# First attention: two of the six additions that sum the weighted shifts are made by GpSimd beside VectorE's next products

## The chip, the cores and the metric

The kernel runs on one core of one Trainium2 chip. The metric is the device time in microseconds, as the median of several runs. The profile is of one execution; its span goes from the first to the last instruction.

## The reference

Two decoder layers with post-norm work on x of 32 sequences by 128 positions by 256 channels: `x = layernorm(x + sublayer(x))`, six times. The sublayers are a windowed attention, a cross attention and routed experts in the first layer, and a decayed attention, a memory attention and a quantized feed-forward network in the second. The change touches the first one:

```
Q, K, V = heads(wq), heads(wk), heads(wv)          # 16 heads of 16 channels
Kw, Vw = Kp[:, :, idx], Vp[:, :, idx]              # 7 shifts, -3 to 3, zero padded
attn = softmax(einsum('bhld,bhlwd->bhlw', Q, Kw) / sqrt(16))
fw = attn * conn                                   # conn: a softmax over the 7 shifts, from weights alone
fw = fw / (fw.sum(-1) + 1e-9)
out = einsum('bhlw,bhlwd->bhld', fw, Vw)
return out @ wo.T + bo
```

So `out` is, for each position, the sum of seven shifted copies of V, each weighted by head.

## The kernel before

The 32 sequences are cut into 16 groups of two. A group's x is 128 positions by 2 x 256 numbers. Each sublayer is a "station", a Python generator that runs once per group on each engine: A (windowed attention, `windowed`), B (`cross`), X (`experts`), C (`decayed`, with the choice of the memory), E (`memory`), F (`feed_forward`); S is the setup. Each `yield` ends a step. The order in which an engine takes the steps of the stations is written out by hand as a string of letters in `ORDER`, one per engine; `walk` goes through it. All instructions of an engine run in this order, so a wait in one step holds up everything behind it. In the middle of the kernel a group is in each station at once: while group 10 is in A, group 7 is in C.

Engines wait for each other by counters (semaphores). `own` is an engine's counter of its own instructions; an instruction that reads what an earlier one on the same engine wrote waits for it.

The first attention on VectorE (`windowed` in the vector block) has these parts. L990 multiplies Q with the seven shifts of K. L1005 to L1023 make the seven weights per head, in `e0`. Then `SUM_STEPS` names 13 steps. A step with one number, as `(3,)`, is L1034: it multiplies the shifted copy `vw[:, wi, :]`, 128 x 512 numbers, with its weights, in place. I call this product wi. A step with two numbers, as `(3, 0)`, is L1038: it adds copy 0 to copy 3. The sum ends up in copy 3 (`PAD`), and the last step raises `a_summed`, for which TensorE's transposes of it (L550) wait. `vw` and all other areas named area_... lie in SBUF; names with bank are in PSUM.

Around these steps in VectorE's queue stand steps of the other stations: of F L1263 and L1257 (two inputs from SBUF), L1284 and L1295 (an input from PSUM); of C the two instructions of L874, which add a bank to x and form the sums for the norm (`n_c.added`); of E L1198 and L1202, for whose result TensorE's next transposes wait.

GpSimd has, besides memsets in the setup, one step per station and group: `scales`, four instructions of 128 x 2 numbers (L1587, L1589, L1591, L1593) that turn the sums (`n.added`, from VectorE) and the squares (`n.squared`, from ScalarE) into the scale and shift of the norm, which ScalarE waits for.

Of the kernel before, what the change touches and what calls it, by code (L numbers as in the profile page):

```python
# [11 lines left out]
ALU = mybir.AluOpType  # L12
# [11 lines left out]
DH = D // H  # L24
# [31 lines left out]
SUM_STEPS = ((3,), (0,), (2,), (3, 0), (4,), (3, 2), (6,), (3, 4), (1,), (3, 6), (5,), (3, 1), (3, 5))  # L56
# [26 lines left out]
        "SAAAAAAASASSSAAAAAAAAAAAAAASSAAAAAABAASSABBAAAAAAAAAAAAAAXSAXSXAAAAASAAXBAXAAAAAAAAAXAAAAABBXSAXXXAAAAAX"  # L83
        "BBAAXBXAAAAAAAACAAAAAXCACAAXCXCAAAAAXEEEEEABABXBAAXEAAAAACAAXAAAACCAAXEECAFCXEEAAAAEFXEFFEBAXFFABAFFXBFF"
        "AFFFXAECFFAAFACCAFXAAAAAAEFAFFAAFEXCAFCFEEXAEAEFAXFAXEBFAFFAABFFXBFAFFFFXAECFFAAFACCAXAFAAAAEAAAAFFFFECX"
        "AFCFEEXAEAFEAXFAXEFBAFFAAFFBXBFAFFFFXAECFFAAFACCAAXFAAAAEAAFAFAFEFCXAFCFEEXAEAFXEAFABFEXAFFAAFFXBBFFAFFF"
        "XAECFFAAAFCCAXFAAAAAEAAAFAFFFEXCAFCFEEXAEAFXEFAAEFAFBFXAAFFXBBFFAFFFXAECFFAAAFCCAXAFAAAAEAAFAFAFFXECAFCF"
        "EEXAEAFXEEFAABXFAFFAAFFXBBFFFAFFXAECFFAAACFCXAAFAAAAEAAAFAFFFXECAFCFEEXAEAFXEFAEAXFFBAFAAFFXBBFFFFAFXAEC"
        "FFAAAFCCAXFAAAAAEAAAFAFFXFECAFCFEEXAEAFEXFAEAXFABAFFAFFXBBFAFFFFXAECFFAAACFCAXFAAAAAEAAAFAFFXFECAFCFEEXA"
        "EAXFEFAAEXFABAFFAFFXBBFAFFFFXAECFFAAACFAXCAFAAAAAEAAAFFXFFECAFCFEEXEAAFEXFAABEFFAAXAFFXFBBFAFFFFXAECFFAA"  # L90
        "AFCCXAFAAAAAEAAAFAFFXFECAFCFEEXEAAFEAXFXAEFABFFAAFFXBBFFAFFFXAEFCAFAAFXCCAFAAAAAEAFAAAFFFXECAFCFEEXEEFXE"
        "FBXFFBFFXFBFFFFFXEFXFFCFCCXEFFFFEFCFCXEEFEEEFFXXFFFCFFFFFXFEXFFCCFXFFFFFEXECFCFEEEEEFFCFFFFCEFCFFFFFFFEF"
        "CFEFCFFFEEFFEEEFFFFFFFFEFFFFFFFEFFFFFEFFFFFFFFFFFFFFFFFFFFFFF"
# [16 lines left out]
        "ABABXABXCABCXEABCEXAFBCEXAFBCEXAFBCEXAFBCXEAFBCXEAFBCXEAFBCEXAFBCXEAFBCEXAFBCXEAFBCXEFCXEFCEFEFF"  # L110
# [43 lines left out]
def build(nc, io, out):  # L154
    ctx = ExitStack()
    with ctx:
# [145 lines left out]
        a_summed, a_values, a_oT, a_wo = sems("a_summed a_values a_oT a_wo")  # L302
# [565 lines left out]
        def _(dve):  # L868
            own = Steps(dve_own)
# [116 lines left out]
            def windowed(g):  # L986
# [43 lines left out]
                for step in SUM_STEPS:  # L1030
                    if len(step) == 1:
                        (wi,) = step
                        v4 = vw[:, wi, :].rearrange("p (b h d) -> p b h d", b=GB, h=H)
                        made[wi] = own.mark(dve.tensor_tensor(v4, v4, bc(e4[:, :, wi, :], 3, DH), ALU.mult))  # L1034
# [546 lines left out]
        def _(pool):  # L1581
# [13 lines left out]
            def windowed(g):  # L1595
                scales(n_a, g).then_inc(n_a.scaled, 1)
                yield
# [120 lines left out]
```

## Time and profile before

| | us |
|---|---|
| median of 3 runs | 1125.49 |
| lowest and highest | 1124.31, 1127.63 |
| span of the profiled execution | 1122.6 |
| busy: TensorE, VectorE, ScalarE, GpSimd | 969.1, 943.0, 750.2, 140.0 |

In the rows PE is TensorE, PEld its weight loads, DVE VectorE, ACT ScalarE, POOL GpSimd. The table by stretches has: the stretch, its length, then for PE, PEld, DVE, ACT and POOL the busy time with the number of instructions, then the granted clock of TensorE as a share of full speed, the share of the DMA engines and GB/s. A row of the view in order of time has: start, duration, engine, line, operation, output and inputs, sizes, how many in a row are merged in it, and in brackets how long the engine was idle before it and what ended that. An instruction may start before the one ahead of it has ended. The chain of work that ended last is followed back from the last instruction, at each step to what released it or to the instruction before it on its engine.

### The profile page before, as it was taken

How to read it: one execution, taken by the hardware profiler on the slowest of the kernel's cores; microseconds unless marked ns; L12 is line 12 of the kernel's file. 1: busy time of each engine (PE TensorE's matmuls, PEld its weight loads, DVE VectorE, ACT ScalarE, POOL GpSimd, SP SyncE). 2: the span in 40 equal slices, each digit the busy share in tenths (PEclk: the TensorE clock that was granted, in tenths of full speed). 3: DMA queues.
4: the chain of work that ended last, by engine and by line, in shares of the span. 5: the costliest groups of instructions: out<-in, count | busy, mean ns of one | idle time of the engine just before them, and what ended most of it. 6: DMA issues, size and time to landing. Idle time of an engine off the chain costs nothing.

```text
span 1122.6 us, 19705 instructions
## 1 busy us (share of the span) xinstructions
PE 969.1 (86%) x7038; PEld 695.0 (62%) x7038; DVE 943.0 (84%) x2503; ACT 750.2 (67%) x1854; POOL 140.0 (12%) x401
## 2 busy tenths in 40 slices
PE   5768879999999999999999999989999888786552
PEld 3545657666767676767676676757576666564331
DVE  4799766689898989899999989898989886868854
ACT  2223454758696878778687868786868786767643
POOL 2000110101111020202020111111020201011000
PEclk8879899999999999999999999999999998999865
DMA  7832023011111212020303020211202000000000
GB/s 205 319 105 75 22 63 94 1 56 30 56 49 38 66 29 75 20 85 10 94 10 94 9 85 11 66 38 39 66 30 66 17 3 20 1 20 1 10 10 10
DMA packets 36626, 58.90 MB, mean 52 GB/s; under 512 B 6784, under 2 KB 15872, under 8 KB 36016
## 3 DMA queue, kind: packets, MB, share of 16 engines
q1 hardware_dynamic: 36528, 57.64, 16.7%
q8 instruction: 56, 0.92, 0.3%
q14 instruction: 42, 0.34, 0.1%
HBM read 28.65 MB, written 4.19 MB: 29 GB/s over the span
## 4 chain that ended last, share of the span: by engine, by line
DVE 52%; PE 31%; ACT 12%; issue 4%; POOL 1%; DMA 0%; SPq 0%; ACTq 0%; DVEq 0%; POOLq 0%
PE bank_c L444 9%; DVE area_f L1248 8%; PE bank_a L444 6%; PE banks_e L444 5%; DVE area_a L990 4%; DVE area_a L1034 4%; DVE neg_top L1181 4%; DVE area_f L1239 3%; DVE x L874 3%; DVE area_a L1038 3%; PE bank_f L444 2%; DVE area_f L1257 2%; PE bank_x L444 2%; ACT squares_out L1322 2%; DVE area_f L1263 2%
## 5 line engine op out<-in xcount | busy, mean ns | idle before, releaser
L1248 DVE SCALAR_TENSOR_TENSOR area_f<-area_f,w_convw 128x254 f32<-128x254 f32 x256 | 111.9, 479 | 10.3 <-ACT area_f L1548 7.8
L1548 ACT ACTIVATE area_f<-area_f,w_convb,w_convw 128x256 f32<-128x256 f32 x128 | 69.8, 594 | 29.1 <-DVE area_f L1239 28.7
L1310 ACT ACTIVATE area_bx<-bank_x 128x512 f32<-128x512 f32 (+1 forms) x144 | 70.0, 498 | 27.1 <-PE bank_x L638 15.6
L990 DVE TENSOR_TENSOR area_a<-area_a 128x512 f32<-128x512 f32 x112 | 73.0, 682 | 14.5 <-ACT area_a L1310 13.7
L1181 DVE TENSOR_REDUCE neg_top<-banks_e 128x8 f32<-128x1024 f32 x64 | 76.1, 1216 | 7.6 <-PE banks_e L444 7.3
L1310 ACT ACTIVATE area_a<-bank_a 128x512 f32<-128x512 f32 (+1 forms) x80 | 44.0, 550 | 49.1 <-PE bank_a L444 33.6
L1310 ACT ACTIVATE area_bx<-bank_c 128x512 f32<-128x512 f32 x64 | 34.5, 539 | 63.0 <-PE bank_c L444 59.9
L1034 DVE TENSOR_TENSOR area_a<-area_a 128x512 f32<-128x512 f32 x112 | 74.3, 684 | 0.4
L1519 ACT ACTIVATE area_e<-banks_e 128x512 f32<-128x512 f32 x128 | 68.6, 594 | 1.4 <-PE banks_e L795 1.4
L1038 DVE TENSOR_TENSOR area_a<-area_a 128x512 f32<-128x512 f32 x96 | 65.7, 684 | 0.3
L444 PE MATMUL bank_x<-area_bx 128*128 128x128 f32 (+1 forms) x256 | 54.8, 348 | 5.7 <-ACT area_bx L1454 4.2
L444 PEld LDWEIGHTS bank_x<-area_bx 128*128 128x128 f32 x256 | 41.2, 194 | 29.7 <-ACT area_bx L1454 13.7
L1310 ACT ACTIVATE area_e<-banks_e 128x512 f32<-128x512 f32 (+1 forms) x80 | 45.5, 589 | 18.8 <-PE banks_e L466 10.1
L1587 POOL TENSOR_SCALAR bn_negmean_b<-bn_sums_b 128x2 f32<-128x2 f32 x16 | 5.1, 316 | 380.0 <-DVE x L874 380.0
L1553 ACT ACTIVATE area_f<-area_f 128x512 f32<-128x512 f32 x64 | 40.7, 636 | 14.1 <-DVE area_f L1248 13.6
L444 PE MATMUL bank_f<-area_f,w1q 128*128 128x256 bf16 x256 | 41.3, 287 | 8.6 <-DVE area_f L1239 7.2
L1239 DVE TENSOR_TENSOR area_f<-bank_f,area_f 128x512 f32<-128x512 f32 x64 | 43.6, 682 | 5.4 <-PE bank_f L444 5.4
L638 PE MATMUL bank_x<-w_wqkv_e,area_bx 128*32 128x384 f32 x512 | 47.9, 492 | 0.0
L1257 DVE SCALAR_TENSOR_TENSOR area_f<-area_f 128x512 f32<-128x512 f32 x64 | 43.8, 685 | 4.6 <-ACT area_f L1553 4.2
L1561 ACT ACTIVATE area_f<-area_f 128x512 f16<-128x512 f32 x64 | 38.7, 629 | 11.2 <-DVE area_f L1295 11.0
L1295 DVE TENSOR_TENSOR area_f<-area_f,bank_f 128x512 f32<-128x512 f32 x64 | 41.1, 680 | 4.0 <-PE bank_f L818 4.0
L444 PE MATMUL banks_e<-area_e,chosen_v 128*32 128x512 f32 x256 | 34.9, 618 | 10.2 <-ACT area_e L1519 10.2
(312 smaller groups left out, 2661.7 us busy)
## 6 DMA issues: line engine op xcount, KB each, us to landing
area_a<-area_a SPq DMA_DIRECT2D x96, 224.0 KB
area_a<-in_xT SPq DMA_DIRECT2D x16, 256.0 KB, 2.9
x<-in_x SPq DMA_DIRECT2D x16, 256.0 KB, 2.8
area_bx<-in_ctxT SPq DMA_DIRECT2D x16, 256.0 KB, 2.7
area_d<-in_ctxT SPq DMA_DIRECT2D x16, 256.0 KB, 2.6
y<-x SPq DMA_DIRECT2D x16, 256.0 KB, 2.2
w_wqkv_e<-in_wqkv_e SPq DMA_DIRECT2D x1, 3072.0 KB, 11.9
area_f<-in_raw SPq DMA_DIRECT2D x2, 1024.0 KB, 9.2
```

Source lines behind the costliest of these rows:

```text
L444: last = pe.matmul(out_ap, l, r, start=i == 0 and not opened, stop=closes and i == len(pairs) - 1)
L638: last = pe.matmul(bank_x[ES * q:ES * (q + 1), 0:3 * HP], xgf[:, c, e, :], wq[:, c, e, :], start=c == 0, stop=c == DC - 1)
L990: return dve.tensor_tensor(product_of(wi).rearrange("p (n t) -> p n t", t=P), qT0.rearrange("p c (b t) -> p (c b) t", t=P), kT0.rearrange( ...
L1034: made[wi] = own.mark(dve.tensor_tensor(v4, v4, bc(e4[:, :, wi, :], 3, DH), ALU.mult))
L1038: added = dve.tensor_tensor(vw[:, to, :], vw[:, to, :], vw[:, wi, :], ALU.add)
L1181: dve.tensor_reduce(top[:, b, :, r:r + 2, 0].rearrange("p (par c) r -> p r c par", c=DC), banks_e[:, r:r + 2, :].rearrange("p r (c par k) ...
L1239: dve.tensor_tensor(blocks(th_f[jj % 3], 2), blocks(bank_f[:, :], 2), bc(tscale_f, 1, 2), ALU.mult).then_inc(f_h, 1)
L1248: last = dve.scalar_tensor_tensor(c4[:, i, :, dst], h4[:, i, :, src], cwt3[:, 2 * jj + i, k:k + 1], c4[:, i, :, dst], ALU.mult, ALU.add)
L1257: dve.scalar_tensor_tensor(c_f[jj], th_f[jj % 3], 1.0, c_f[jj], ALU.add, ALU.mult).then_inc(f_silu, 1)
L1310: return act.activation(dst, src, ACT.Copy)
L1519: act.activation(pT_e[:, r * 4 * P:(r + 1) * 4 * P], bank_e[r][:, :], ACT.Exp, scale=float(DH) ** -0.5).then_inc(e_exp, 1)
L1548: last = act.activation(c4[:, i], h4[:, i], ACT.Identity, bias=w["convb"][:, j:j + 1], scale=cwt3[:, j, 1:2])
```

## The change

Additions 0 <- 0 + 2 and 4 <- 4 + 6 move to GpSimd (`POOL_STEPS`). VectorE makes the products in another order, counts products 2 and 6 on a new semaphore `a_weighted`, and keeps four additions, (3, 1), (3, 5), (3, 0), (3, 4). The last two take in what GpSimd has added and wait for a second new semaphore, `a_paired`. VectorE's string loses two letters A per group and GpSimd's gains two. The strings of the other engines stay.

```diff
-SUM_STEPS = ((3,), (0,), (2,), (3, 0), (4,), (3, 2), (6,), (3, 4), (1,), (3, 6), (5,), (3, 1), (3, 5))
+SUM_STEPS = ((0,), (2,), (4,), (6,), (3,), (1,), (3, 1), (5,), (3, 5), (3, 0), (3, 4))
+POOL_STEPS = ((0, 2), (4, 6))
...
     "POOL": (
-        "ABABXABXCABCXEABCEXAFBCEXAFBCEXAFBCEXAFBCXEAFBCXEAFBCXEAFBCEXAFBCXEAFBCEXAFBCXEAFBCXEFCXEFCEFEFF"
+        "AAABAAAAABXABAAXCABAACXEABACAEXAFBACAEXAFBACAEXAFBACAEXAFBACAXEAFBACAXEAFBACAXEAFBACAEXAFBACAXEAFBACAEXA"
+        "FBACAXEAFBCXEFCXEFCEFEFF"
...
-                        made[wi] = own.mark(dve.tensor_tensor(v4, v4, bc(e4[:, :, wi, :], 3, DH), ALU.mult))
+                        weighted = dve.tensor_tensor(v4, v4, bc(e4[:, :, wi, :], 3, DH), ALU.mult)
+                        if wi in (2, 6):
+                            weighted.then_inc(a_weighted, 1)
+                        elif wi not in (0, 4):
+                            made[wi] = own.mark(weighted)
                     else:
                         to, wi = step
-                        dve.wait_ge(own.sem, max(made[to], made[wi]))
+                        if wi in (0, 4):
+                            dve.wait_ge(own.sem, made[to])
+                            dve.wait_ge(a_paired, 2 * g + (1 if wi == 0 else 2))
+                        else:
+                            dve.wait_ge(own.sem, max(made[to], made[wi]))
...
             def windowed(g):
+                for i, (to, wi) in enumerate(POOL_STEPS):
+                    pool.wait_ge(a_weighted, 2 * g + i + 1)
+                    pool.tensor_tensor(vw[:, to, :], vw[:, to, :], vw[:, wi, :], ALU.add).then_inc(a_paired, 1)
+                    yield
                 scales(n_a, g).then_inc(n_a.scaled, 1)
                 yield
```

Lines of the changed kernel are numbered 2 to 10 higher: L1034 becomes L1036, L1038 L1048, L874 L876, L1198 L1208, L1263 L1273. Three places show the order, all of group 10. VectorE, the first three products and what stands behind them, after:

```order
L1036 TENSOR_TENSOR area_a<-area_a 128x512 [waits a_fw,shift_in]
L1036 TENSOR_TENSOR area_a<-area_a 128x512 x2
L1152 RECIPROCAL area_c<-area_c 128x2 [waits c_exp]
L1273 TENSOR_TENSOR area_f<-area_f 128x512 [waits dve_own,f_abs]
L876 SCALAR_TENSOR_TENSOR x,bn_sums_c<-bank_c,area_c,x 128x256 [waits c_pv,dve_own]
```

Before, the same rows stand there under their old line numbers, but the three products were those of copies 3, 0, 2. Now they are of 0, 2, 4, and the second releases the first addition on GpSimd.

VectorE, from the second reciprocal to L1198, before:

```order
L1038 TENSOR_TENSOR area_a<-area_a 128x512 [waits dve_own]
L1034 TENSOR_TENSOR area_a<-area_a 128x512
L1284 TENSOR_REDUCE area_f<-bank_f 128x2 [waits f_topT]
L1286 TENSOR_SCALAR area_f<-area_f 128x2 [waits dve_own]
L1288 RECIPROCAL area_f<-area_f 128x2 [waits dve_own]
L1290 TENSOR_SCALAR area_f<-area_f,wmean 128x2 [waits dve_own]
L1291 TENSOR_SCALAR area_f<-area_f 128x2
L1038 TENSOR_TENSOR area_a<-area_a 128x512 [waits dve_own]
L1034 TENSOR_TENSOR area_a<-area_a 128x512
L1038 TENSOR_TENSOR area_a<-area_a 128x512 [waits dve_own]
L1034 TENSOR_TENSOR area_a<-area_a 128x512
L1198 RECIPROCAL area_e<-banks_e 128x16 [waits e_back]
```

And after:

```order
L1036 TENSOR_TENSOR area_a<-area_a 128x512
L1294 TENSOR_REDUCE area_f<-bank_f 128x2 [waits f_topT]
L1296 TENSOR_SCALAR area_f<-area_f 128x2 [waits dve_own]
L1298 RECIPROCAL area_f<-area_f 128x2 [waits dve_own]
L1300 TENSOR_SCALAR area_f<-area_f,wmean 128x2 [waits dve_own]
L1301 TENSOR_SCALAR area_f<-area_f 128x2
L1036 TENSOR_TENSOR area_a<-area_a 128x512 x2
L1048 TENSOR_TENSOR area_a<-area_a 128x512 [waits dve_own]
L1208 RECIPROCAL area_e<-banks_e 128x16 [waits e_back]
L1212 TENSOR_TENSOR area_e<-banks_e,area_e 128x8x16 [waits dve_own]
```

Two additions have gone from this stretch, and one, (3, 1), stands right behind product 1. The second row with L1036 of the after piece stands for two products, 3 and 1.

GpSimd, stations B and C, before:

```order
L1593 TENSOR_TENSOR bn_scale_b<-bn_negmean_b,bn_scale_b 128x2 [waits pool_own]
L1587 TENSOR_SCALAR bn_negmean_c<-bn_sums_c 128x2 [waits c_added]
L1589 TENSOR_SCALAR bn_scale_c<-bn_squares_c 128x2 [waits c_squared]
L1591 TENSOR_TENSOR bn_scale_c<-bn_scale_c,halves 128x2 [waits pool_own]
L1593 TENSOR_TENSOR bn_scale_c<-bn_negmean_c,bn_scale_c 128x2 [waits pool_own]
```

And after, where area_a is `vw`:

```order
L1603 TENSOR_TENSOR bn_scale_b<-bn_negmean_b,bn_scale_b 128x2 [waits pool_own]
L1608 TENSOR_TENSOR area_a<-area_a 128x512 [waits a_weighted]
L1597 TENSOR_SCALAR bn_negmean_c<-bn_sums_c 128x2 [waits c_added]
L1599 TENSOR_SCALAR bn_scale_c<-bn_squares_c 128x2 [waits c_squared]
L1601 TENSOR_TENSOR bn_scale_c<-bn_scale_c,halves 128x2 [waits pool_own]
L1603 TENSOR_TENSOR bn_scale_c<-bn_negmean_c,bn_scale_c 128x2 [waits pool_own]
L1608 TENSOR_TENSOR area_a<-area_a 128x512 [waits a_weighted]
```

The first addition stands between the scales of B and C, the second behind the scales of C.

## Rows read from the trace of the kernel before

**Rows 1.** The page, part 1: busy time of the engines

```profile
PE 969.1 (86%) x7038; PEld 695.0 (62%) x7038; DVE 943.0 (84%) x2503; ACT 750.2 (67%) x1854; POOL 140.0 (12%) x401
```

**Rows 2.** Table by stretches of the periods of groups 4 and 10

```profile
209.00:269.00 60.00, 56.49 (x415) 40.87 (x413) 47.58 (x130) 40.48 (x106) 6.93 (x20) 0.97 0.14 40
...
569.00:629.00 60.00, 57.61 (x439) 41.85 (x438) 56.28 (x151) 46.77 (x117) 8.60 (x24) 1.00 0.17 49
```

**Rows 3.** The chain from 269 to 869 us, shares by line

```profile
by line: DVE area_f L1248 11.0%; DVE area_a L990 6.8%; DVE neg_top L1181 6.4%; DVE area_a L1034 5.9%; PE bank_c L444 5.5%; PE bank_a L444 5.3%; PE banks_e L444 4.4%; issue 4.3%; DVE area_f L1239 4.0%; DVE area_a L1038 3.2%; DVE area_f L1257
```

**Rows 4.** VectorE in order of time, groups 9 and 10 (start us, us, instruction)

```profile
509.29 1.89 DVE L1034 TENSOR_TENSOR area_a<-area_a 128x512 f32<-128x512 f32 x3
...
569.12 1.89 DVE L1034 TENSOR_TENSOR area_a<-area_a 128x512 f32<-128x512 f32 x3
...
571.01 0.67 DVE L1263 TENSOR_TENSOR area_f<-area_f 128x512 f32<-128x512 f32 x1
...
572.00 0.48 DVE L874 SCALAR_TENSOR_TENSOR x<-bank_c,area_c,x 128x256 f32<-128x256 f32 x1
...
572.48 0.67 DVE L1038 TENSOR_TENSOR area_a<-area_a 128x512 f32<-128x512 f32 x1
...
574.93 0.16 DVE L1291 TENSOR_SCALAR area_f<-area_f 128x2 f32<-128x2 f32 x1
575.00 0.68 DVE L1038 TENSOR_TENSOR area_a<-area_a 128x512 f32<-128x512 f32 x1
575.60 0.68 DVE L1034 TENSOR_TENSOR area_a<-area_a 128x512 f32<-128x512 f32 x1
```

**Rows 5.** The chain after the sums of group 10, in order of time

```profile
577.69 0.50 DVE area_e L1202 x2
...
578.89 1.73 PE bank_c L444 x8
...
591.93 1.20 PE banks_e L444 x16
```

**Rows 6.** VectorE in order of time, end of group 1

```profile
77.49 0.68 DVE L1034 TENSOR_TENSOR area_a<-area_a 128x512 f32<-128x512 f32 x1
78.09 1.41 DVE L1038 TENSOR_TENSOR area_a<-area_a 128x512 f32<-128x512 f32 x2
```

**Rows 7.** GpSimd in order of time, group 10

```profile
572.58 0.63 POOL L1587 TENSOR_SCALAR bn_negmean_c<-bn_sums_c 128x2 f32<-128x2 f32 x1 [8.34 <-DVE x L874]
...
574.80 0.20 POOL L1593 TENSOR_TENSOR bn_scale_c<-bn_negmean_c,bn_scale_c 128x2 f32<-128x2 f32 x1
```

**Rows 8.** Groups of instructions on GpSimd: its two larger memsets

```profile
L1623 POOL MEMSET area_a<- 128x3584 f32 x1 | 3.1, 3088 | 0.0
L1622 POOL MEMSET area_a<- 128x536 f32 x1 | 0.5, 544 | 0.0
```

**Rows 9.** The same view: first instruction of the scales, stations A and C

```profile
L1587 POOL TENSOR_SCALAR bn_negmean_c<-bn_sums_c 128x2 f32<-128x2 f32 x16 | 8.2, 513 | 168.2 <-DVE x L874 168.2
...
L1587 POOL TENSOR_SCALAR bn_negmean_a<-bn_sums_a 128x2 f32<-128x2 f32 x16 | 3.1, 191 | 67.5 <-DVE x L874 67.5
```

**Rows 10.** All engines in order of time, group 15

```profile
874.66 0.74 POOL L1589 TENSOR_SCALAR bn_scale_c<-bn_squares_c 128x2 f32<-128x2 f32 x1 [1.30 <-ACT squares_out L1322]
874.66 0.68 DVE L1034 TENSOR_TENSOR area_a<-area_a 128x512 f32<-128x512 f32 x1
...
875.26 0.68 DVE L1038 TENSOR_TENSOR area_a<-area_a 128x512 f32<-128x512 f32 x1
```

**Rows 11.** All engines in order of time, group 4

```profile
213.29 1.42 DVE L1038 TENSOR_TENSOR area_a<-area_a 128x512 f32<-128x512 f32 x2
...
216.11 0.20 POOL L1593 TENSOR_TENSOR bn_scale_c<-bn_negmean_c,bn_scale_c 128x2 f32<-128x2 f32 x1
...
216.50 0.42 DVE L874 SCALAR_TENSOR_TENSOR x<-bank_x,x 128x256 f32<-128x256 f32 x1 [1.80 <-PE bank_x L444]
```

**Rows 12.** All engines in order of time, group 8

```profile
453.98 0.69 POOL L1591 TENSOR_TENSOR bn_scale_c<-bn_scale_c,halves 128x2 f32<-128x2 f32 x1
...
454.36 0.69 DVE L1034 TENSOR_TENSOR area_a<-area_a 128x512 f32<-128x512 f32 x1
```

More of the change, by code:

```diff
@@ L82 @@
     "DVE": (
[L83 to L92, printed above, removed]
@@ L93 @@
-        "CFEFCFFFEEFFEEEFFFFFFFFEFFFFFFFEFFFFFEFFFFFFFFFFFFFFFFFFFFFFF"
+        "SAAAAAAASASSSAAAAAAAAAAAASSAAAAAABAASSABBAAAAAAAAAAAAXSAXSXAAAAASAAXBAXAAAAAAAXAAAAABBXSAXXXAAAAAXBBAAXB"
+        "XAAAAAACAAAAAXCACAAXCXCAAAAAXEEEEEABABXBAAXEAAAACAXAAAACCAAXEECAFCXEEAAAAEFXEFFEBAXFFABAFFXBFFAFFFXAECFF"
+        "AAFACCFXAAAAAEFAFFAAFEXCAFCFEEXAEAEFAXFAXEBFAFFAABFFXBFAFFFFXAECFFAAFACCXAFAAAEAAAAFFFFECXAFCFEEXAEAFEAX"
+        "FAXEFBAFFAAFFBXBFAFFFFXAECFFAAFACCAXFAAAEAAFAFAFEFCXAFCFEEXAEAFXEAFABFEXAFFAAFFXBBFFAFFFXAECFFAAAFCCXFAA"
@@ new lines @@
+        "AAEAAAFAFFFEXCAFCFEEXAEAFXEFAAEFAFBFXAAFFXBBFFAFFFXAECFFAAAFCCXAFAAAEAAFAFAFFXECAFCFEEXAEAFXEEFAABXFAFFA"
+        "AFFXBBFFFAFFXAECFFAAACFCXAFAAAEAAAFAFFFXECAFCFEEXAEAFXEFAEAXFFBAFAAFFXBBFFFFAFXAECFFAAAFCCXFAAAAEAAAFAFF"
+        "XFECAFCFEEXAEAFEXFAEAXFABAFFAFFXBBFAFFFFXAECFFAAACFCXFAAAAEAAAFAFFXFECAFCFEEXAEAXFEFAAEXFABAFFAFFXBBFAFF"
+        "FFXAECFFAAACFXCAFAAAAEAAAFFXFFECAFCFEEXEAAFEXFAABEFFAAXAFFXFBBFAFFFFXAECFFAAAFCCXFAAAAEAAAFAFFXFECAFCFEE"
+        "XEAAFEAXFXAEFABFFAAFFXBBFFAFFFXAEFCAFAAFXCCFAAAAEAFAAAFFFXECAFCFEEXEEFXEFBXFFBFFXFBFFFFFXEFXFFCFCCXEFFFF"
@@ L94 @@
+        "EFCFCXEEFEEEFFXXFFFCFFFFFXFEXFFCCFXFFFFFEXECFCFEEEEEFFCFFFFCEFCFFFFFFFEFCFEFCFFFEEFFEEEFFFFFFFFEFFFFFFFE"
+        "FFFFFEFFFFFFFFFFFFFFFFFFFFFFF"
     ),
@@ L301, in build @@
         a_turned, a_shifted, a_exp, a_fw = sems("a_turned a_shifted a_exp a_fw")
-        a_summed, a_values, a_oT, a_wo = sems("a_summed a_values a_oT a_wo")
+        a_weighted, a_paired, a_summed, a_values, a_oT, a_wo = sems("a_weighted a_paired a_summed a_values a_oT a_wo")
         b_proj, b_kav, b_xT, b_xT_out, b_scores, b_top, b_exp, b_turned, b_pT, b_pv = sems(
```

## Prediction

> **What bounds the kernel now.** I began with the busy times. TensorE is busy for 969.1 us of a span of 1122.6, VectorE for 943.0, ScalarE for 750.2, and GpSimd for 140.0 [rows 1]. Two engines are near full and one is almost empty, so a change that takes work from VectorE and gives it to GpSimd touches the right engine, provided that GpSimd can do it beside VectorE. The table by stretches says when VectorE is the limit: over the period of 60 us that holds the first attention of group 10 it is busy for 56.28 us, at a granted clock of 1.00 [rows 2]. Ten such periods lie in the trace and the eight from 269 to 749 us read alike.
>
> Next I read the chain of work that ended last. Over the 600 us from 269 to 869 it runs through L1034 (the weighted shifts) for 5.9% and through L1038 (the additions) for 3.2% [rows 3]. That is 54.6 us. The 11 groups in that stretch have 77 products and 66 additions at 0.60 us from start to start [rows 4], 86 us in all, so about two thirds of these steps are on the chain. The piece of the chain in [rows 5] shows which: it leaves VectorE at L1202 and stays on TensorE for 15 us, until 593.13. What stands ahead of L1198 and L1202 in VectorE's queue is on the chain. In group 10 that is nine of the thirteen steps. The last four run while TensorE is the bound.
>
> **What is taken away.** Two of six additions per group leave VectorE. One lasts 0.68 us, but the next instruction starts 0.60 us after it (575.00 to 575.60 [rows 4]), so one is worth 0.60 us. The order of before has nine steps ahead of L1198, that of after has seven ahead of L1208, as this line is numbered there. So the full 1.20 us a group comes off the chain, not two thirds of it.
>
> **What the new order adds on VectorE.** An addition that needs the product right ahead of it can't overlap it. The pair of additions at the end of a group shows the price: two take 1.41 us and one 0.68, so the second starts 0.73 us after the first where independent steps have 0.60 [rows 6]. It costs 0.13 us. Before, in group 10, no addition stands right behind what it needs. After, there are three such places, of which one, (3, 1), is ahead of L1208. I count +0.13 us on the chain and leave 0.26 us to the part that TensorE hides; its cover is the stay of the chain on TensorE, and without it the 16 groups would pay another 4 us. The counter a_weighted replaces an increment of VectorE's own and costs nothing there.
>
> **What GpSimd costs by itself.** It has room: it stands idle for 8.34 us ahead of the scales of station C's norm in this group [rows 7]. No row shows an addition of 128x512 on it. The nearest are its two memsets, 3088 ns for 3584 elements and 544 ns for 536 [rows 8]: 2544 ns for 3048 elements, 0.835 ns each, or 0.43 us for one pass over 512. The addition reads twice and writes once. The bounds for the time in which it reads are one pass, 0.43 us, and three, 1.28 us. Two passes are 0.85 us. I take 1.07, halfway between two and three, because reads and writes may not overlap fully, and keep both ends.
>
> **What it costs VectorE.** This is the term on which the sign rests. In the trace, a GpSimd instruction on two elements takes 191 ns when nothing disturbs it [rows 9]. When a VectorE instruction with two inputs from SBUF is in flight, it waits until that has ended: next to the L1038 of 572.48 to 573.15 the same instruction starts at 572.58 and takes 0.63 us [rows 4, 7]; next to the L1034 of 874.66 to 875.34, a scale takes 0.74 us and ends at 875.40 [rows 10]. The mean of the 16 for station C, which usually meet an L1038, is 513 ns [rows 9]. So both engines read through something that one of them holds for a whole instruction. GpSimd gets its turn at the first boundary, although VectorE's next instruction has already started by then: at 875.26, before the scale ended [rows 10]. That next instruction lost nothing, but GpSimd read two elements there, not 1024.
>
> The Trainium skill (SBUF — State Buffer, section "SBUF: two separate sides") calls this a pair of ports shared by VectorE and GpSimd, locked for a whole instruction by whoever starts first, with the loser fully blocked. By that rule the trace agrees for one direction (0.63 us instead of 0.19); that VectorE is blocked by GpSimd, no row of before shows.
>
> I assume that it goes both ways. Nearly all that surrounds the GpSimd additions on VectorE has two SBUF inputs. The first one is released by product 2. Product 4 is then in flight until 571.01; GpSimd reads from there to about 572.08. After a reciprocal, VectorE has L1263, which starts at 571.01 [rows 4] and would be held for 1.07 us. The second addition is queued behind the four scale instructions of station C's norm. Those end 2.5 us after the norm's sums (572.48 to 575.00 [rows 4, 7]). By that time, with one addition fewer ahead, VectorE has product 3 in flight (574.40 to 575.08), so GpSimd reads from there, and product 1 is held for 1.07 us. Both places are ahead of L1208, on the chain.
>
> The sum for a group is −1.20 + 0.13 + 2 x 1.07 = **+1.07 us**. I count the 11 groups from 269 us on in full (11.8). For the five before I count a fifth (1.1), since VectorE has slack there (47.58 us of 60 in the period of group 4 [rows 2]). Sum +12.9, as if 12 groups counted. The profiled execution has 1122.6 us, the median of the runs 1125.49; the 2.9 us between them lie around the span and stay. Forecast: **1138 us**.
>
> The skill has a figure for the addition itself (GPSIMD Engine Reference, section "3.1 Elementwise — side-by-side cycle accounting"): about 2.6 cycles an element at 1.2 GHz for two inputs, since they share one read port. An estimate from it is 1.11 us for 512. No run here shows it, and the sum would be about 1 us higher by it.
>
> **The new waits.** VectorE's (3, 0) and (3, 4) wait for a_paired. Behind them in its queue stand L1305 and the norms of other stations. In group 10 the second addition on GpSimd ends near 576.3 and (3, 4) starts after 580, 3.5 us later, so nothing waits. The one tight place is group 4, where station C's norm comes just before (3, 0) and (3, 4): its scales end at 216.31 [rows 11], the addition about 1.1 us later, and (3, 4) would start at about 214. The next norm there waits for TensorE until 216.50 anyway, so this costs at most about 1.5 us, once. On GpSimd the four scales of station C's norm are now queued behind the first addition; this ends before their input is there.
>
> **Rivals.**
> (a) GpSimd holds nothing against VectorE, or only for a moment. For it: in [rows 12] an L1034 starts in the middle of a GpSimd instruction of 0.69 us and takes its usual 0.69. Against it: that instruction had long read its two elements. Then a group gets −1.20 + 0.13 = −1.07 us; times 12 that is −13, so 1113 us, and down to 1108 if all 16 groups count. This ends on the other side. It decides from a hold of 0.53 us per addition: below that the change gains.
> (b) The hold is about one pass. −1.20 + 0.13 + 0.86 is −0.21 us a group, −3 for 12 groups, 1123 us: no difference.
> (c) The hold is long. With three passes it is 1.28: +1.49 us a group, 18 for 12 groups and 24 for 16, so 1143 to 1149 us. A GpSimd addition that waits for more than one VectorE instruction, and so slides towards (3, 4), would belong here too: it turns 3.5 us of margin into a wait of VectorE.
> (d) The removed additions were not on the chain. Then gain and loss are both small, within 2 or 3 us. Against it speaks [rows 5].
>
> **Chances.** The hold goes both ways with two or three passes, 1133 to 1143 us: 0.52. (c) beyond that: 0.09. (b) and (d): 0.18. (a): 0.21. A measurement of this kernel can tell about 0.3%, or 3.4 us, from no change. Slower by more than that: 0.60; within: 0.19; faster: 0.21. The range for 8 in 10 leaves out the far end of (a) and of (c): 1112 to 1147.
>
> **What the profile of the changed kernel would show.** If I am right: 32 GpSimd additions of about 1.1 to 1.3 us, longer when product 4 or 3 is in flight as they start; an L1273 and a product (L1036) per group that take about 1.7 us instead of 0.68; all other VectorE instructions as before; VectorE's busy time up by some 12 us, if a held instruction is recorded as a long one, although it runs 32 instructions fewer; the period, 59.8 us from the first product of group 9 at 509.29 to that of group 10 at 569.12 [rows 4], up to about 60.9. If (a) holds, no two-input instruction on VectorE is longer than 0.70 us and the period falls to 58.7. I am wrong in the size if the lengthened instructions gain other than 1.1 us each, and wrong in the place if VectorE idles at (3, 4) or the scales of station C's norm come late.

## The result, and the profile after

The changed kernel is slower: 1142.88 us median against 1126.56 for the kernel before on the same chip, a ratio of 1.0142 with a 95% interval of 1.012 to 1.0164. The forecast was 1138 us, between 1112 and 1147, with slower at 0.60. The profiled execution has a span of 1139.9 us where before had 1122.6, so 17.3 us were added.

The first view is the page's part on busy times. The columns are busy us, share of the span and number of instructions.

```profile
PE 978.1 (86%) x7038; PEld 697.9 (61%) x7038; DVE 957.9 (84%) x2471; ACT 751.7 (66%) x1854; POOL 191.9 (17%) x433
```

Against [rows 1] GpSimd took over 32 instructions and 52 us. VectorE runs 32 fewer and is busy 14.9 us longer (the forecast had some 12). The work was not carried off, it was made dearer. The groups of instructions by line say where (count, then busy us and mean ns of one):

```profile
L1036 DVE TENSOR_TENSOR area_a<-area_a 128x512 f32<-128x512 f32 x112 | 83.9, 790 | 0.4
...
L1048 DVE TENSOR_TENSOR area_a<-area_a 128x512 f32<-128x512 f32 x64 | 54.5, 851 | 1.6
...
L1273 DVE TENSOR_TENSOR area_f<-area_f 128x512 f32<-128x512 f32 x48 | 41.2, 859 | 2.5 <-ACT area_f L1567 2.5
```

```profile
L1608 POOL TENSOR_TENSOR area_a<-area_a 128x512 f32<-128x512 f32 x32 | 50.1, 1567 | 125.7 <-DVE area_a L1036 125.7
```

L1036 is the products, L1048 the additions, L1273 a step of station F. An undisturbed one of any of them takes 0.68 us (L992 and L1267 beside them have means of 682 and 684 ns). So some are much longer. The order of time in group 10 shows which. VectorE and GpSimd, start and duration in us:

```profile
578.44 1.89 DVE L1036 TENSOR_TENSOR area_a<-area_a 128x512 f32<-128x512 f32 x3
580.25 0.16 DVE L1152 RECIPROCAL area_c<-area_c 128x2 f32<-128x2 f32 x1
580.33 1.70 DVE L1273 TENSOR_TENSOR area_f<-area_f 128x512 f32<-128x512 f32 x1
581.95 0.47 DVE L876 SCALAR_TENSOR_TENSOR x<-bank_c,area_c,x 128x256 f32<-128x256 f32 x1
...
584.75 1.29 DVE L1036 TENSOR_TENSOR area_a<-area_a 128x512 f32<-128x512 f32 x2
586.08 1.65 DVE L1048 TENSOR_TENSOR area_a<-area_a 128x512 f32<-128x512 f32 x1
587.64 0.24 DVE L1208 RECIPROCAL area_e<-banks_e 128x16 f32<-128x16 f32 x1
```

```profile
579.81 1.66 POOL L1608 TENSOR_TENSOR area_a<-area_a 128x512 f32<-128x512 f32 x1 [6.23 <-DVE area_a L1036]
582.92 0.63 POOL L1597 TENSOR_SCALAR bn_negmean_c<-bn_sums_c 128x2 f32<-128x2 f32 x1 [1.44 <-DVE x L876]
...
585.15 0.34 POOL L1603 TENSOR_TENSOR bn_scale_c<-bn_negmean_c,bn_scale_c 128x2 f32<-128x2 f32 x1
585.45 1.72 POOL L1608 TENSOR_TENSOR area_a<-area_a 128x512 f32<-128x512 f32 x1
```

The first addition starts at 579.81, while the third product runs until 580.33, and ends at 581.47. The reciprocal passes unharmed. The L1273 of 580.33 takes 1.70 us. Then station C's norm (L876) starts, at 581.95, where by the rows of before it came 2.47 us after the first product and now comes 3.51. The second addition starts at 585.45 and the L1048 of 586.08 takes 1.65 us instead of 0.68. VectorE is never idle in front of an addition that waits for a_paired. In the whole trace, 29 of the 32 GpSimd additions lengthen one VectorE operation by 0.96 to 1.12 us. One in group 4 does so by 0.32. Two do nothing; one of these, in group 3, has the L1146 (an input from PSUM) and a reduction beside it.

### The profile page after: what moved, and what is told of

Same layout as the page of the kernel before. It is cut to its first block, busy times and chain, and to the rows that moved or that the text cites. A ratio compares the mean times of both kernels' runs of the same rounds, so it can differ in the third digit from the quotient of the medians.

```text
span 1139.9 us, 19737 instructions
## 1 busy us (share of the span) xinstructions
PE 978.1 (86%) x7038; PEld 697.9 (61%) x7038; DVE 957.9 (84%) x2471; ACT 751.7 (66%) x1854; POOL 191.9 (17%) x433
## 4 chain that ended last, share of the span: by engine, by line
DVE 53%; PE 28%; ACT 12%; issue 5%; POOL 1%; DMA 0%; SPq 0%; ACTq 0%; DVEq 0%; POOLq 0%
DVE area_f L1258 8%; PE bank_c L446 7%; PE bank_a L446 6%; DVE area_a L1036 5%; DVE area_a L992 4%; PE banks_e L446 4%; DVE neg_top L1191 4%; DVE area_a L1048 3%; DVE area_f L1249 3%; DVE x L876 2%; PE bank_f L446 2%; DVE area_f L1267 2%; ACT squares_out L1332 2%; PE bank_x L446 2%; DVE area_f L1273 2%
## 5 line engine op out<-in xcount | busy, mean ns | idle before, releaser
L992 DVE TENSOR_TENSOR area_a<-area_a 128x512 f32<-128x512 f32 x112 | 73.0, 682 | 14.5 <-ACT area_a L1320 13.6
L1036 DVE TENSOR_TENSOR area_a<-area_a 128x512 f32<-128x512 f32 x112 | 83.9, 790 | 0.4
L1608 POOL TENSOR_TENSOR area_a<-area_a 128x512 f32<-128x512 f32 x32 | 50.1, 1567 | 125.7 <-DVE area_a L1036 125.7
L1048 DVE TENSOR_TENSOR area_a<-area_a 128x512 f32<-128x512 f32 x64 | 54.5, 851 | 1.6
L1267 DVE SCALAR_TENSOR_TENSOR area_f<-area_f 128x512 f32<-128x512 f32 x64 | 43.8, 684 | 4.8 <-ACT area_f L1563 4.3
```

Source lines behind the costliest of these rows:

```text
L992: return dve.tensor_tensor(product_of(wi).rearrange("p (n t) -> p n t", t=P), qT0.rearrange("p c (b t) -> p (c b) t", t=P), kT0.rearrange( ...
L1036: weighted = dve.tensor_tensor(v4, v4, bc(e4[:, :, wi, :], 3, DH), ALU.mult)
L1048: added = dve.tensor_tensor(vw[:, to, :], vw[:, to, :], vw[:, wi, :], ALU.add)
L1267: dve.scalar_tensor_tensor(c_f[jj], th_f[jj % 3], 1.0, c_f[jj], ALU.add, ALU.mult).then_inc(f_silu, 1)
L1608: pool.tensor_tensor(vw[:, to, :], vw[:, to, :], vw[:, wi, :], ALU.add).then_inc(a_paired, 1)
```

## One period in three pieces

A period of the steady groups runs from the first product of a group to that of the next. I cut it at two VectorE instructions: the start of station C's norm (L876, L874 before) and the reciprocal L1208 (L1198 before), behind which the chain goes over to TensorE. For before the chain has both:

```profile
569.12 1.89 DVE area_a L1034 x3
...
571.59 0.89 DVE x L874 x4
...
577.49 0.18 DVE area_e L1198
```

That is 2.47 and 5.9 us for group 10. Each number of the three pieces is the median of groups 6 to 10 of one profiled execution (us); the last columns are the mean period of groups 5 to 14, the time from the first product of group 0 to that of group 5, and what lies behind the first product of group 15. The kernels are those of the experiments below.

| kernel | product to norm C | norm C to L1208 | L1208 to product | mean period | groups 0 to 4 | rest |
|---|---|---|---|---|---|---|
| before | 2.60 | 5.82 | 51.42 | 59.90 | 239.9 | 254.3 |
| after | 3.68 | 5.71 | 51.56 | 61.02 | 243.6 | 256.9 |
| all steps on VectorE, new order | 2.60 | 5.94 | 51.59 | 60.17 | 239.1 | 255.5 |
| additions on 2 columns | 2.60 | 5.66 | 51.58 | 59.84 | 235.8 | 255.3 |
| additions on 256 columns | 3.13 | 5.66 | 51.59 | 60.32 | 239.6 | 256.7 |
| first addition alone | 3.68 | 5.66 | 51.57 | 60.75 | 238.9 | 258.2 |
| second addition alone | 2.60 | 5.71 | 51.57 | 60.10 | 239.7 | 256.2 |
| zeros written | 2.60 | 5.66 | 51.58 | 59.83 | 234.2 | 256.8 |
| one input read | 3.01 | 5.66 | 51.59 | 60.21 | 237.1 | 257.4 |
| first behind C's scales | 2.60 | 5.71 | 51.94 | 60.74 | 243.3 | 259.6 |
| both beside norm C | 3.20 | 5.66 | 52.25 | 61.47 | 238.4 | 258.0 |

The experiments are what fills this table; the readings follow with them. Each row is one execution, and not all that differs between rows comes from the change. The time up to the first product of group 0 is not in the table: it is 29.3 us before, 29.1 after, but 33.7 with the first addition alone and 34.2 with both beside norm C. In groups 0 to 4 the kernels of experiments 6 and 8 run the same instructions as before and have 238.4 to 239.8 us, so that column is good to about 1.5 us.

## The experiments

**1. Additions on 2 of 512 columns.** Everything of the change stays except the size of what GpSimd reads.

```diff
-pool.tensor_tensor(vw[:, to, :], vw[:, to, :], vw[:, wi, :], ALU.add)...
+pool.tensor_tensor(vw[:, to, 0:2], vw[:, to, 0:2], vw[:, wi, 0:2], ALU.add)...
```

> Left out: the two additions on GpSimd cover 2 of the 512 columns; instruction order, counters and waits are those of the changed kernel. Theory H (GpSimd's reading holds up the next VectorE instruction with two SBUF inputs for about 1.1 us, 29 times): no such VectorE instruction is longer than 0.70 us, GpSimd's take 0.19 to 0.6 us, and the time falls by some 30 us against the changed kernel, to 1110 to 1116 us, below the kernel before. Rival O (the new order and the queueing on GpSimd cost the time): the time stays above 1135 us.

Measured: 1122.21 us, a ratio of 0.9969 (0.995 to 0.9987). The hold is gone, as expected: no VectorE operation is lengthened. But the gain of the two removed additions is not there either. I had expected 1110 to 1116. The piece from norm C to L1208 fell from 5.82 to 5.66 and not by 1.07 to 4.75. VectorE in order of time, group 11:

```profile
628.13 0.48 DVE L876 SCALAR_TENSOR_TENSOR x<-bank_c,area_c,x 128x256 f32<-128x256 f32 x1
...
632.64 0.69 DVE L1048 TENSOR_TENSOR area_a<-area_a 128x512 f32<-128x512 f32 x1
633.79 0.26 DVE L1208 RECIPROCAL area_e<-banks_e 128x16 f32<-128x16 f32 x1 [0.46 <-PE banks_e L473]
```

Now VectorE waits there for TensorE. The chain of group 10 shows the other path:

```profile
569.62 1.22 PE bank_c L446 x8
570.84 0.99 PE banks_e L446 x8
571.83 1.93 PE bank_x L446 x8
573.76 0.45 PE banks_e L473 x4
...
574.23 0.27 DVE area_e L1208
```

Those four pieces of TensorE's work take 4.6 us without a gap, and L1208 needs the last of them. They start 1.04 us after norm C starts (at 568.58 in this group). So this piece of the period can't be shorter than some 5.65 us, whatever is taken from VectorE. Before stood 0.17 above that floor. VectorE's wait ahead of L1208 is 0.82 us in groups 6, 7, 9 and 10 and 0.30 to 0.46 in the other steady ones; in groups 8, 11, 12 and 14 it has also waited 0.26 to 0.40 at L1294 for TensorE's bank_f. So four groups of ten could take 0.82 us more on VectorE in this piece without loss, and the rest 0.30 to 0.46.

**2. All steps on VectorE, in the new order.** What the order alone costs.

```diff
-SUM_STEPS = ((3,), (0,), (2,), (3, 0), (4,), (3, 2), (6,), (3, 4), (1,), (3, 6), (5,), (3, 1), (3, 5))
+SUM_STEPS = ((0,), (2,), (4,), (0, 2), (6,), (3,), (4, 6), (1,), (3, 1), (5,), (3, 5), (3, 0), (3, 4))
```

> The kernel before with its thirteen steps all on VectorE, in a sequence of products and additions that has the changed kernel's pairings and its additions right behind the step they need, (3, 1), (3, 5), (3, 0), (3, 4); nothing is left out. If a place where an addition stands right behind what it needs costs 0.13 us, and only the part ahead of L1198 counts: +2 to +3 us for 16 groups, 1128 to 1130 us. If all of them are on the chain: up to +6, 1133 us. If the spacing costs nothing: 1126 us.

Measured: 1128.34 us, ratio 1.0042 (1.0021 to 1.0062), as expected. The table shows where: +0.12 between norm C and L1208, the price of one dependent pairing, and +0.17 behind L1208. That second piece is in every kernel that has the new order, also where GpSimd adds 2 columns (51.58).

**3. Additions on 256 columns.**

```diff
-pool.tensor_tensor(vw[:, to, :], vw[:, to, :], vw[:, wi, :], ALU.add)...
+pool.tensor_tensor(vw[:, to, 0:T], vw[:, to, 0:T], vw[:, wi, 0:T], ALU.add)...
```

> Left out: the additions on GpSimd cover 256 of 512 columns. If the hold goes with what GpSimd reads, the VectorE instruction behind it is longer by 0.53 to 0.6 us instead of 1.08, the GpSimd addition takes about 0.7 us alone instead of 1.26, and the time lies halfway between e1_tiny and the changed kernel, 1126 to 1130 us. If the hold is a fixed price per instruction: 1138 us or more.

Measured: 1130.03 us, ratio 1.005 (1.003 to 1.0069), at the upper end of what was expected. GpSimd's addition takes 720 to 731 ns alone, where 512 columns take 1261 to 1273. The product or L1273 that the first addition holds takes 1214 to 1221 ns, and less, as here, where a reciprocal stands ahead of it. Group 10:

```profile
572.43 1.15 DVE L1273 TENSOR_TENSOR area_f<-area_f 128x512 f32<-128x512 f32 x1
573.50 0.47 DVE L876 SCALAR_TENSOR_TENSOR x<-bank_c,area_c,x 128x256 f32<-128x256 f32 x1
```

The hold is 0.53 us for 256 columns and 1.07 for 512: 2.1 ns a column, and nothing fixed. The piece from the first product to norm C grew by just that, 2.60 to 3.13, and the period by 0.42. This was the first sign that in the steady groups the first addition sets most of the loss.

**4. Only the first, only the second addition at full size.** This tells what each hold costs.

```diff
+n = W2 if i == 0 else 2        # the other kernel: if i == 1
-pool.tensor_tensor(vw[:, to, :], vw[:, to, :], vw[:, wi, :], ALU.add)...
+pool.tensor_tensor(vw[:, to, 0:n], vw[:, to, 0:n], vw[:, wi, 0:n], ALU.add)...
```

> The changed kernel with GpSimd's first addition of a group as it is (512 columns) and the second on 2 columns only, so that the weighted sum lacks most of its summand. Theory P (what runs on is the first addition's hold, because it lies ahead of station C's norm, while the freed time of the two removed additions lies behind it where TensorE's turn for the banks of station E is as late): period of the steady groups 60.6 to 60.9, about as in the changed kernel, 1137 to 1142. Theory S (the sum of the prediction: each hold 1.07, the removed additions -1.20 in full, the second hold gone): period about 59.7 - 1.20 + 0.13 + 1.07 = 59.7 a group, 1124 to 1128.

> The changed kernel with GpSimd's second addition of a group as it is and the first on 2 columns only (the sum lacks most of that summand). Theory P (the second hold lies behind station C's norm, where the freed 1.20 covers it): period 59.7 to 59.9, 1121 to 1126. Theory S gives 1124 to 1128 as for the first alone; what tells the two apart is that by S the two kernels take the same time and by P this one is 13 to 18 us below the other.

Measured: with the first alone 1139.33 us, ratio 1.0098 (1.0067 to 1.0129); with the second alone 1130.41 us, ratio 1.0038 (1.0018 to 1.0058). By the sum of the prediction the two would be alike. They are 8.9 us apart, less than the 13 to 18 that theory P had, since the second alone came out above its 1121 to 1126.

The two profiled spans are 11.5 us apart, of which 6.5 lie in the ten steady periods, 2.0 behind the first product of group 15, −0.8 in groups 0 to 4, and 3.8 ahead of the first product of group 0, where there is no hold yet. So the total overstates the difference, and the periods carry the argument. The three pieces of the second alone (2.60, 5.71, 51.57) add up to 59.88, yet its mean period is 60.10: groups 5, 8 and 11 to 14 have 6.07 to 6.46 in the middle piece. These are the groups in which, by experiment 1, VectorE has only 0.30 to 0.46 us to spare ahead of L1208.

The chain of group 10 with the first alone:

```profile
579.77 0.90 DVE x L876 x4
...
580.80 1.22 PE bank_c L446 x8
582.02 0.99 PE banks_e L446 x8
583.02 1.93 PE bank_x L446 x8
584.94 0.45 PE banks_e L473 x4
...
585.42 0.27 DVE area_e L1208
```

Here the chain passes through norm C, which came 1.03 late in this group, and goes by TensorE; the sums on VectorE are off it. VectorE sits idle for 0.82 us ahead of L1208. With the second alone VectorE has no wait there, and the chain runs through the lengthened addition:

```profile
576.73 1.65 DVE area_a L1048
578.38 0.18 DVE area_e L1208
```

The two additions that VectorE lost (1.20), the dependent pairing (0.13) and this hold (0.96) give 5.71 from 5.82, as measured. So against before the freed time pays for the whole second hold in groups 6, 7, 9 and 10, and in most others for part of it. Against the kernel without holds (59.84) the first alone adds 0.91 us to the mean period, the second 0.26, both together 1.18. In groups 0 to 4, where both stand among products, the two are nearly alike: about 3 and 4 us, 8 together.

**5. Other work of GpSimd in the same place.** Does GpSimd hold VectorE by running, or by reading?

```diff
-pool.tensor_tensor(vw[:, to, :], vw[:, to, :], vw[:, wi, :], ALU.add)...
+pool.memset(vw[:, to, :], 0.0)...
```

> The two GpSimd additions of each group replaced by GpSimd writing 512 columns of zeros to the same place (no input is read; the weighted sum then lacks these parts). Is it the GpSimd instruction as such that holds VectorE, or its reading from SBUF? By reading: no VectorE operation is lengthened (products stay at 684 ns), the write takes 0.4 to 0.6 us, the period stays at 59.7 as with the additions on 2 columns, 1120 to 1124. By the instruction as such: a product or addition behind each write takes 0.9 to 1.2 us.

```diff
-pool.tensor_tensor(vw[:, to, :], vw[:, to, :], vw[:, wi, :], ALU.add)...
+pool.tensor_scalar(vw[:, to, :], vw[:, to, :], 2.0, None, ALU.mult)...
```

> The two GpSimd additions of each group replaced by a GpSimd multiplication of the same 512 columns by a constant (one input read instead of two; two of the seven weighted shifts are then left out of the sum). If the hold is the reading of two inputs together, none is seen and VectorE's products stay at 684 ns, 1120 to 1125. If any GpSimd reading holds the port for as long as the instruction streams, VectorE's operation behind takes 684 ns plus 0.4 to 0.6 us, that is 1.1 to 1.3 us, and the period lies near that of the additions on 256 columns, 60.15, 1128 to 1132.

Measured, one run each: 1120.83 and 1128.3 us. GpSimd and VectorE in group 10 of the kernel that writes zeros, and then VectorE and GpSimd of the kernel that reads one input:

```profile
564.62 0.52 POOL L1608 MEMSET area_a<- 128x512 f32 x1 [6.22 <-DVE area_a L1036]
...
565.15 0.67 DVE L1273 TENSOR_TENSOR area_f<-area_f 128x512 f32<-128x512 f32 x1
```

```profile
570.38 1.02 DVE L1273 TENSOR_TENSOR area_f<-area_f 128x512 f32<-128x512 f32 x1
```

```profile
569.88 1.87 POOL L1608 TENSOR_SCALAR area_a<-area_a 128x512 f32<-128x512 f32 x1 [6.26 <-DVE area_a L1036]
```

Writing holds nothing and doesn't wait: the 32 writes take 517 to 528 ns with a product in flight. Reading one input holds VectorE's products for 0.41 us (1097 to 1100 ns instead of 684 for the first of a group; the L1273 shown, behind a reciprocal, has 0.34), although GpSimd's instruction itself is longer than the addition, 1.49 us where nothing is in flight ahead of it. What counts is what GpSimd reads, not how long it runs. And 0.41 is what the piece ahead of norm C grew by (2.60 to 3.01).

So with a first hold of 0, 0.41, 0.53 and 1.07 us the piece ahead of norm C has 2.60, 3.01, 3.13 and 3.68. It enters in full.

**6. Both additions beside work that reads PSUM.** From group 5 on both are released by product 6 and meet station C's norm, a reciprocal and a reduction from PSUM; in groups 0 to 4 all sums stay on VectorE.

```diff
+FIRST = 5
...
-SUM_STEPS = ((0,), (2,), (4,), (6,), (3,), (1,), (3, 1), (5,), (3, 5), (3, 0), (3, 4))
+SUM_STEPS = ((0,), (2,), (4,), (6,), (3,), (1,), (5,), (3, 0), (1, 5), (3, 4), (3, 1))
...
-pool.wait_ge(a_weighted, 2 * g + i + 1)
+pool.wait_ge(a_weighted, g - FIRST + 1)
```

> Nothing is left out. From group 5 on both GpSimd additions are released together by product 6, all four products stand ahead of the part of VectorE's queue in which nothing has two SBUF inputs (L1142, the norm of station C, L1125, L1284 to L1291, together some 2.3 us), and the scales of station C come behind both additions on GpSimd; groups 0 to 4 keep all six additions on VectorE. Theory H: two additions need about 2.5 us, so no VectorE instruction is longer by more than 0.3 us; the 1.2 us a group are gained and some 0.2 given back: 10 us less than before, 1114 to 1118 us. Rival O: the norm of station C is late by 0.6 to 1.6 us per group and takes the gain: 1124 to 1135 us. If also instructions with one SBUF input or a PSUM input are held: 1140 us.

Measured: 1140.78 us, ratio 1.0136 (1.0115 to 1.0157). This is outside both 1114 to 1118 and 1124 to 1135. It meets the 1140 of the third case by number, but the chain below gives another cause. The placing did what it should: the two additions take 1.26 to 1.28 us each, and no operation with two SBUF inputs is lengthened. But four scale instructions of station C's norm are queued behind them on GpSimd, and these became the chain:

```profile
582.05 2.49 POOL area_a L1612 x2
584.54 0.16 POOL bn_negmean_c L1601
...
585.04 1.22 POOL bn_scale_c L1605
...
586.33 0.63 POOL bn_scale_c L1607
...
586.99 0.60 ACT x L1342
```

The negative mean starts at 584.54, over a microsecond after the norm's sums, and the third scale instruction (L1605) takes 1.22 us, since the next products of VectorE hold GpSimd in turn. The hold was traded for a queue. A second cost is in the table: four products instead of three now stand ahead of norm C, and that piece has 3.20 us instead of 2.60, by just one product (0.60). I had not counted it, and how the 1.57 us by which the mean period grew divide between the two was not measured. A small surprise stands on VectorE in the same place:

```profile
582.97 0.67 DVE L1298 TENSOR_REDUCE area_f<-bank_f 128x2 f32<-128x512 f32 x1
583.68 0.89 DVE L1300 TENSOR_SCALAR area_f<-area_f 128x2 f32<-128x2 f32 x1
```

L1300 works on two elements a partition and takes 0.89 us; the same step takes 0.18 in the kernels where GpSimd is quiet. It ends with GpSimd's addition. The reduction from PSUM beside it is not touched.

**7. The first addition behind station C's scales.** Only its place in GpSimd's order moves, from group 5 on.

```diff
-... "ACAEXAFBACAEXAFB..."
+... "CAAEXAFBCAAEXAFB..."
```

> The changed kernel with nothing altered but the place of GpSimd's first addition from group 5 on: it is issued behind station C's scales, directly ahead of the second one. Both additions run at full size, so both holds are there as before, but now both lie behind station C's norm. Theory P: the first hold no longer delays the norm. The freed 1.20 covers one hold of 1.07 behind the norm (the run with the second addition alone kept a period of 59.8 to 60.0), a second one there finds at most 0.2 to 0.5 of cover: period 60.3 to 60.9, 1132 to 1141, at or below the changed kernel. If there is more slack behind the norm than the freed time: 59.8 to 60.2, 1126 to 1131. By the prediction's sum, which counts holds wherever they lie: 60.8, 1140 to 1143. If the later first sum makes the pairing (3,0) wait, or the second addition moves station E's scales: above 61, over 1143.

Measured: 1138.44 us, ratio 1.01 (1.0076 to 1.0124). The hold ahead of norm C is gone (2.60 again), so from group 6 to 10 the first products stand 60.3, 60.3, 61.2 and 60.2 us apart, 242.0 in all where the changed kernel has 244.6. Then it loses: in the steady groups the second addition now meets L1208 and L1212, which read PSUM, and lengthens only the product behind them, by 0.39 us:

```profile
584.56 1.64 DVE L1048 TENSOR_TENSOR area_a<-area_a 128x512 f32<-128x512 f32 x1
586.13 0.24 DVE L1208 RECIPROCAL area_e<-banks_e 128x16 f32<-128x16 f32 x1
586.41 0.49 DVE L1212 TENSOR_TENSOR area_e<-banks_e,area_e 128x128 f32<-128x128 f32 x2
586.81 1.07 DVE L1036 TENSOR_TENSOR area_a<-area_a 128x512 f32<-128x512 f32 x1
```

Those 0.39 us are behind L1208, where I took the chain to be on TensorE. The last piece grew by 0.37 all the same (51.57 to 51.94). So the cover that I had counted on behind L1208 is not there. The chain of group 9 shows the other path, out of the last steps on VectorE over ScalarE to TensorE:

```profile
530.94 0.61 DVE area_f L1305
...
531.57 0.63 ACT area_f L1571
532.20 0.49 ACT area_a L1320
...
532.74 0.39 PE bank_a L458
```

L458 starts 6.68 us behind L1208 here. With the second addition alone it starts 6.29 behind it, after TensorE has been idle for 0.03, and before the change 6.21 behind it, without a wait. So in this group the new order alone uses the cover up, and each further delay of the sums is paid. In groups 5 and 12 both holds were whole and ahead of L1208, and these periods are 62.7 and 61.3 us. So this version is ahead of the changed kernel in its middle groups, and no gain against before. Its median fell inside the 1132 to 1141 of theory P, but the cover behind the norm was less even than either theory had it.

**8. Products instead of additions.** In search of a better version: before, with two or one of the seven Q x K products on GpSimd, behind station F's scales, from group 6 on; VectorE skips these.

```diff
+POOLED, FIRST = 2, 6        # the other kernel: 1, 6
...
+pool.wait_ge(a_qkv, 3 * g + 2)
+for wi in WINDOWS[:POOLED]:
+    last = pool.tensor_tensor(product_of(wi)..., qT0..., kT0..., ALU.mult)
+last.then_inc(a_pooled, 1)
```

> The kernel before (all sums on VectorE), with two of the seven Q x K products of each group from group 6 on made by GpSimd, behind station F's scales, where VectorE reduces the banks of station E from PSUM. Each GpSimd product takes 1.26 alone; K is copied by ScalarE until 597.5 in group 10, so the two would run from 597.6 to 600.1, beside VectorE's scan and small products (598.29 to 599.0) and one reduction of PSUM. If the second finds VectorE on the PSUM reduction and the first holds only the scan (at most 1.1), VectorE gets 1.2 less work and up to 1.1 of hold a group: 1120 to 1126. If TensorE or the chain by station C's exp sets the period anyway, nothing is gained: 1124 to 1127. If the second product ends later than VectorE's own would (600.1 against 599.6 of before) or holds a product too, +0.3 to +1.0 a group over 10 groups: 1128 to 1136.

> As the kernel with two products on GpSimd, but with one: GpSimd's work ends at 598.9, as VectorE's first product would begin, so nothing waits for it. It takes 0.61 from VectorE and holds the scan or the small product by 0.3 to 1.0. No change in the period if the freed time is again not on the binding path (1124 to 1127); 1119 to 1123 if VectorE's work sets the products' end; above 1129 if the hold is on the path in full.

Measured: 1130.21 us, ratio 1.0037 (1.0023 to 1.0052), and 1130.47, ratio 1.0032 (1.0009 to 1.0054). I had put two products at 1120 to 1126 if the hold caught only the scan, and at 1128 to 1136 if they ended late; they ended at 600.68, as in the second case. VectorE beside them:

```profile
598.82 0.81 DVE L1089 TENSOR_SCALAR area_bx<-area_bx 64x128 f32<-64x128 f32 x1
599.66 1.30 DVE L1091 TENSOR_TENSOR_SCAN area_bx<-onesb,area_bx 64x128 f32<-64x128 f32 x1
```

The first product held the L1089 (0.81 instead of 0.22 us), the second the scan (1.30 instead of 0.42). MATCH_REPLACE8 (0.27 us at 598.51) passes as if GpSimd were not there. For one product the profiled span was 1122.1 us, 0.5 below before, while the ratio of its runs is 0.3% above. That median, 1130.47, lies in the worst of the three cases I had put down (above 1129), though the mean period of the profiled execution is only 0.1 us longer than before. None of these kernels beats before.

## Why the prediction was right, and where it was not

**The hold.** The likeliest case was that GpSimd's reading holds VectorE for 1.07 us an addition, both ways. It does: 1.06 to 1.09 behind a product, 1.02 for the L1273 behind a reciprocal, 1.12 where GpSimd starts just ahead of an L1048, and 0.96 for the L1048 behind a product, which would have waited 0.13 us for its own input anyway. That the value halfway between two and three passes hit it so closely was luck; the bounds were sound. The Trainium skill (SBUF — State Buffer, section "SBUF: two separate sides") has the pair of ports locked in both directions; the direction that no row of before could show is shown by the L1273 of 580.33. The Trainium skill's figure of 2.6 cycles an element at 1.2 GHz (GPSIMD Engine Reference, section "3.1 Elementwise — side-by-side cycle accounting") gives an estimate of 1.11 us for 512, and two sizes here, 1266 and 725 ns, differ by 2.1 ns a column, 2.5 such cycles.

**The victims.** The first was the L1273, as forecast. For the second I had named product 1, with GpSimd taking its turn after product 3. The second addition got its turn one operation later, at the end of product 1, and held (3, 1), the L1048 of 586.08. The first hold is not the reason: with the second addition alone the same L1048 of group 10 is held. The reason is a wait that the forecast had named and then not applied: the last of the four scale instructions found product 3 in flight, waited for its end (0.34 us at 585.15 instead of the 0.20 of before), and by then product 1 had started (585.36). The price was nearly the same, and the place still ahead of L1208.

**The full 1.20 us off the chain.** This step fails. With the holds gone, the piece that holds the removed additions shrank by 0.16 us and not by 1.07, since TensorE's own 4.6 us of work between norm C and L1208 is almost as long. [rows 5] was read too quickly: that the chain leaves VectorE at L1202 says what ended last, not how far behind the next path was, and that distance was 0.17 us. In the sum nothing shows of it, because the second hold fell into the same piece and used the freed time up: −1.20 + 0.13 + 1.07 is 0.0 by the forecast, and 5.82 to 5.71 by the table. That the two sizes met was luck.

What was wrong is the price of the rivals. A kernel without any hold would not be at 1113 us, as (a) had it; experiments 1 and 5 put it at 1121 to 1122. Rival (d), that the removed additions were not on the chain, was right about their worth, and (a) would have ended there. Rival (b), a hold of 0.43 at 1123 us, has a near match in the one-input read of experiment 5, 0.41 at 1128.3 in one run. The range went 9 us lower than any kernel without a hold came to. One count was off too: the 600 us from 269 to 869 hold the sums of ten groups and not of eleven, 78 us, so that some 70% of these steps were on the chain.

**The dependent pairings.** One was counted at 0.13 on the chain; experiment 2 has +0.12 in that piece. The other two, 0.26, were left to TensorE's cover. The piece behind L1208 grew by 0.14 in the changed kernel and by 0.17 in experiment 2, so this cover is only partial.

**The sum for a period.** Forecast: −1.20 + 0.13 + 1.07 + 1.07 = +1.07. Measured: +1.08 ahead of norm C, −0.11 to L1208, +0.14 behind it, +1.11 by medians and +1.12 as the mean of ten periods, 11.2 us in all.

**The number of groups.** Here the forecast came out low. Groups 0 to 4 were counted at a fifth each, 1.1 us, by VectorE's slack in the period of group 4. They cost 3.7. Group 3 does cost nothing (51.4 us to the next first product in both kernels), and group 4 costs 0.1; but groups 0, 1 and 2 cost 1.6, 1.2 and 0.8, and there an addition less is also worth the most: experiment 1 gains 4.0 us in them. These are differences of two single executions, with the 1.5 us of doubt named under the table. The stretch of group 4 was taken for all five. Group 15 and what follows cost 2.6 where 1.1 was counted; the new order alone has 1.2 of that. Together 3.7 + 11.2 + 2.6, less 0.2 at the start, is the 17.3 us by which the span grew, against 12.9.

**The new waits.** None of them showed. VectorE is not idle at (3, 0) or (3, 4), and station C's scales start within 1 us of the norm's first sum as before.

What stays open: how much of the loss after group 15 comes from which order, what sets the time up to the first product, which differs by some 5 us between executions, and how the loss of experiment 6 divides between the queue and the fourth product.

## What to carry to other kernels

GpSimd is no free second VectorE for fp32 work in SBUF: where VectorE's operations beside it have two SBUF inputs, each column of its addition is taken from them, here 2.1 ns a column against the 1.2 ns (0.60 us for 512) that VectorE would need itself. Before a gain is counted for work taken off the chain, the next path's distance has to be read: make the work vanish, or shorten it to two columns, and see which wait appears. And equal costs are not paid equally: two equal holds less than 6 us apart added 0.91 and 0.26 us to the mean period. The first lies ahead of norm C, from which both paths start, so both are late by it; the second lies on one path alone, and is paid only beyond the room that this path has, which differed from group to group. That the chain has gone over to another engine is no cover by itself: a hold of 0.39 us behind L1208 was paid almost in full.

## What the runs showed of the hardware

- A GpSimd addition of 128x512 fp32 takes 1.26 to 1.27 us alone and holds VectorE for 1.07; of 128x256, 0.72 to 0.73 and 0.53; of 128x2, nothing measurable. If a VectorE operation with two SBUF inputs is in flight, GpSimd waits for its end and then takes 1.13 us more, although VectorE's next operation has already started. Once, in group 5 of the kernel with the first addition alone, it waited for the end of the next one too (2.27 us) and then held nothing, since reads of PSUM, a reciprocal and a reduction stood behind.
- A GpSimd operation with one input of 512 columns holds for 0.41 us while it takes 1.49. A GpSimd write of zeros (0.52 us) neither holds nor waits.
- Held on VectorE: products and additions with both inputs in SBUF, the scan, and, which I had not expected, TENSOR_SCALAR on SBUF (0.89 instead of 0.18 us on 128x2, 0.81 instead of 0.22 on 64x128). Not held: RECIPROCAL (0.16 us at 582.90 in experiment 6, inside an addition), MATCH_REPLACE8 (0.27), reductions (0.42 from SBUF, 0.67 from PSUM), and operations with an input from PSUM (L878 of experiment 6, 0.48).
